# Group norm and attention over 4096 positions: the running score maxima of a chunk folded from 1024 to 256 columns before the block turn

## The reference

```python
def _L0_conv_ref(x, Wq, Wk, Wv, gamma):
    f = jnp.einsum('qc,bcn->bqn', Wq, xf)          # 64 x N
    g = jnp.einsum('qc,bcn->bqn', Wk, xf)          # 64 x N
    h = jnp.einsum('vc,bcn->bvn', Wv, xf)          # 256 x N
    scores = jnp.einsum('bqn,bqm->bnm', f, g)      # N x N
    beta = jax.nn.softmax(scores, axis=1)          # over n
    o = jnp.einsum('bvn,bnm->bvm', h, beta)
    return gamma[0] * o + xf
x = x + _L0_conv_ref(_gn(x), ...)                  # _gn: group norm, 32 groups
```

## Time and profile before

| | before |
|---|---|
| median of 3 runs | 1927.47 us (1927.34 to 1928.86) |
| the profiled execution | 1927.25 us, span of its records 1925.5 us |
| TensorE clock granted | 1.000 of full speed over the span |
| busy share of the span | PE 98%, DVE 82%, ACT 82%, POOL 68% |
| block turn, L873 | 64 instructions of 128 x 1024, 79.1 us |
| reduction, L878 | 64 instructions of 128 x 1024, 76.0 us |

### The profile page before, as it was taken

How to read it: one execution, slowest core, us unless ns; L and a number is a source line. 1 busy time by engine, 2 the same in 40 slices (tenths; PEclk the granted TensorE clock), 3 DMA queues, 4 the chain that set the end, 5 groups by cost and what they waited for, 6 DMA issues and landing times.

```text
span 1925.5 us, 44218 instructions
## 1 busy us (share of the span) xinstructions
PE 1895.5 (98%) x17497; PEld 1566.5 (81%) x17497; DVE 1587.3 (82%) x1923; ACT 1571.8 (82%) x1677; POOL 1307.2 (68%) x765
## 2 busy tenths in 40 slices
PE   6899999999999999999999999999999999999999
PEld 3678888878888888887888888888788888888888
DVE  7888998887778899987777989998777787888784
ACT  4788889977778888897877888898787788888885
POOL 4367668866656677886654766788575567766777
PEclk9999999999999999999999999999999999999999
DMA  4022112212111221211211211121130111111111
GB/s 144 4 68 77 45 33 74 56 23 64 32 41 55 74 54 28 73 53 32 60 36 40 71 52 54 53 56 45 28 72 24 23 31 32 32 25 31 32 31 37
DMA packets 200110, 91.19 MB, mean 47 GB/s; under 512 B 150240, under 2 KB 191712, under 8 KB 199904
## 3 DMA queue, kind: packets, MB, share of 16 engines
q1 hardware_dynamic: 199904, 88.36, 17.6%
HBM read 46.60 MB, written 16.78 MB: 33 GB/s over the span
## 4 chain that ended last, share of the span: by engine, by line
PE 93%; issue 0%; ACT 0%; DVE 0%; POOL 0%; DVEq 0%
PE O L515 23%; PE O L517 23%; PE O L516 23%; PE S L503 7%; PE S L500 7%; PE S L497 6%; PE O L474 1%; PE O L476 1%; PE O L475 1%; PE S L526 1%; PE O L460 1%; PE O L459 1%; PE O L464 1%; PE S L474 0%; PE S L475 0%
## 5 line engine op out<-in xcount | busy, mean ns | idle before, releaser
L400 POOL TENSOR_TENSOR PL<-SC,PH 128x1024 f16<-128x1024 f32 x511 | 1089.2, 2137 | 562.1 <-ACT SC L669 558.7
L515 PE MATMUL O<-V,PH 128*128 128x257 f16 x4096 | 1118.3, 273 | 1.2 <-POOL PL L428 1.1
L517 PE MATMUL O<-V,PL 128*128 128x257 f16 x4096 | 1118.2, 273 | 0.0
L516 PE MATMUL O<-V,PH 128*128 128x256 f16 x4096 | 1116.4, 273 | 0.0
L668 ACT ACTIVATE PH<-SC 128x1024 f16<-128x1024 f32 x511 | 539.1, 1055 | 119.0 <-PE O L517 110.8
L907 DVE TENSOR_TENSOR SC<-SC,MB 128x1024 f32<-128x1024 f32 x511 | 613.1, 1209 | 0.1
L662 ACT ACTIVATE SC<-S 128x1024 f32<-128x1024 f32 x512 | 502.8, 1013 | 117.6 <-issue 105.5
L867 DVE TENSOR_TENSOR XM<-S,XM 128x1024 f32<-128x1024 f32 x384 | 468.0, 1219 | 125.6 <-PE S L503 124.2
L669 ACT ACTIVATE SC<-SC 128x1024 f32<-128x1024 f32 x511 | 533.3, 1044 | 0.0
L515 PEld LDWEIGHTS O<-V,PH 128*128 128x128 f16 x4096 | 406.0, 99 | 49.8 <-POOL PL L428 1.3
L516 PEld LDWEIGHTS O<-V,PH 128*128 128x128 f16 x4096 | 400.8, 98 | 50.0
(11 more groups left out here) (126 smaller groups left out, 1076.1 us busy)
## 6 DMA issues: line engine op xcount, KB each, us to landing
xin<-x SPq DMA_DIRECT2D x24, 1024.0 KB, 5.6
xres<-x SPq DMA_DIRECT2D x64, 256.0 KB, 2.9
ATT<-OT SPq DMA_DIRECT2D x1008, 16.0 KB, 1.9
out<-RES SPq DMA_DIRECT2D x63, 256.0 KB, 2.2
SC<-x SPq DMA_DIRECT2D x8, 512.0 KB, 7.4
F<-GG SPq DMA_DIRECT2D x64, 64.0 KB, 2.0
GG<-GG SPq DMA_DIRECT2D x32, 128.0 KB, 2.4
SC<-wvT SPq DMA_DIRECT2D x1, 256.0 KB, 6.8
```

Source lines behind the costliest of these rows:

```text
L400: pool.tensor_tensor(PL[:, s % RING, :], sc(s), PH[:, s % RING, :], ALU.subtract).then_inc(pl_ready, 1)
L515: mm(o[:, 0:C + 1], PH[:, n % RING, cols], vh, start=t == 0, stop=False)
L516: mm(o[:, 0:C], PH[:, n % RING, cols], vl, start=False, stop=False)
L517: w = mm(o[:, 0:C + 1], PL[:, n % RING, cols], vh, start=False, stop=t == T - 1)
```

## The change

The 1024 columns of XM are folded in place by two elementwise maxima: columns 0 to 511 with 512 to 1023, then 0 to 255 with 256 to 511. Both inputs and the output of each lie in SBUF. Behind each fold DVE waits for its own result, by a new semaphore `mx_folded`. The turn then covers 256 columns instead of 1024, the tensor MT has 256 columns instead of 1024, and the reduction goes over 256 columns (32 for each of the 8 outputs) instead of 1024.

```diff
-        MT = sb("MT", [P, GW], f32)
+        MT = sb("MT", [P, M], f32)
...
+        mx_folded = sem("mx_folded")
...
             def turn_maxima(c):
                 dve.wait_ge(s_maxed, G * (c + 1))
                 if c > 0:
                     dve.wait_ge(mxq_ready, c)
-                ve.transpose(MT[:, :], XM[:, :]).then_inc(mx_turned, 1)
+                for i, w in enumerate((GW // 2, M)):
+                    ve.tensor_tensor(XM[:, 0:w], XM[:, 0:w], XM[:, w:2 * w], ALU.max).then_inc(mx_folded, 1)
+                    dve.wait_ge(mx_folded, 2 * c + i + 1)
+                ve.transpose(MT[:, :], XM[:, 0:M]).then_inc(mx_turned, 1)
 
             def quadrant_maxima(c):
 
                 dve.wait_ge(mx_turned, c + 1)
-                ve.tensor_reduce(mxq, MT[:, :].rearrange("p (i j n) -> p j i n", i=GT, j=NB), axis=AX.XY,
+                ve.tensor_reduce(mxq, MT[:, :].rearrange("p (j n) -> p j n", j=NB), axis=AX.X,
                                  op=ALU.max).then_inc(mxq_ready, 1)
```

## The result

| | before | after |
|---|---|---|
| median | 1927.47 us | 2024.92 us (2018.46 to 2028.23, 6 runs) |
| ratio, 95% interval | | 1.0501 (1.0482 to 1.0519) |
| the profiled execution | 1927.25 us, span 1925.5 | 2028.23 us, span 2026.5 |
| TensorE clock granted, mean | 1.000 | 0.988 |

The change makes the kernel 97 us slower, 5.0%; the forecast was 2014 us.

What follows compares the result with a forecast made beforehand. PE's own work was taken to bound the kernel. Boundary stalls of 37 + 31 + 20 us, less 0.9 in the opening, made 87 us on 1927.25 us: forecast 2014 us, range 1938 to 2050 us.

Steps and rivals of the forecast that it cites:

- What bounds, and where it breaks: PE's own work sets the time; a late DVE hurts first at the boundary between two chunks, at the wait for `scale_output`.
- the slack: At a chunk boundary, `scale_output`'s first half may be 1.44 us later before PE waits; 0.75 us at the six coefficient boundaries.
- The wait for POOL: On DVE, a fold waits for the rest of whatever POOL instruction is running; the bounds were nothing and that rest.
- The argument from L847: L847, with SBUF input and output, took 2.29 us instead of 0.80 behind a running POOL instruction; folds should wait likewise.
- The handover: Between the folds, POOL's waiting instruction (2.14 us at plain boundaries) gets in, and fold 2 ends about 0.22 us after it.
- plain: 44 boundaries where POOL starts L400 0.24 us after the turn began; PE stalls 0.84 us each, 37 us in all.
- 12 normalising: Boundaries where POOL runs a pair of L424, 2.12 us each, from -0.20; PE stalls 2.55 us each, 31 us in all.
- 6 coefficient: Chunks 5 and 6 of three batches, POOL's first L400 beginning 0.07 before the turn; stall 3.39 us each, 20 us.
- Fold 2 keeps its turn: Rival: DVE's next instruction precedes the waiting POOL instruction, so the folds run together; 16 us slower, 1943 us; chance 0.17.
- no wait at all: Rival: folds do not wait for POOL, PE never stalls, only the -0.9 us is left; 1926 us; chance 0.14.
- POOL's queue first: Rival: at the 12 normalising boundaries each fold lets one more POOL instruction of 2.1 us pass; 2064 us; chance 0.06.
- The gain of 0.9 us forecast for the opening: Chunks 0 and 1, where PE waits for the first weights: shorter turn and reduction save 0.45 us each.

Runs made afterwards that it cites:

- delay experiments: Kernel before, with two or four extra reductions of XM as pure delay ahead of each turn from chunk 2 on: 1989.98 us and 2235.96 us.
- the last experiment: Changed kernel with POOL held back for the turn, plus two extra reductions of MT, 0.39 us each, ahead of the real one: 1927.70 us, ratio 1.0005.
- the delay kernel: Kernel before, with two extra reductions of XM to 8 columns as pure delay ahead of each turn from chunk 2 on: 1989.98 us, ratio 1.0326.

## Why the prediction was right, point by point

**What bounds, and where it breaks.** Right. PE had 81.6 us of waits for `scale_output` at 59 boundaries, and at the other three the same wait, put down to L916 (1.9 us); none elsewhere of note. The delay experiments show that the place and the slack hold for delays of 2.4 and 4.9 us that have nothing to do with folds.

**The wait for POOL.** Right, and shown: same length and same place, 418 ns with one input in PSUM, up to 2354 with both in SBUF; holding POOL back brings both folds to 0.71 and 0.43 us. The argument from L847 led to the right end of the bounds. Its reason was looser than the fact: the runs show that one SBUF input goes free in a maximum (and in every reduction tried), and two wait. L847, which has one SBUF input and waited all the same, is another operation (a tensor_scalar), and no run here takes its case apart. The sentence of the Trainium skill, in SBUF — State Buffer, section "Who interferes with whom", that two SBUF inputs contend with a GpSimd instruction that reads SBUF, agrees with this pair of runs. The other half of what the prediction took from the Trainium skill there, that whichever starts first holds the ports for its whole length, agrees too, but for the edge: POOL got in some 0.15 us before the end of fold 1's record.

**The handover.** Right: fold 2 lost its turn to a POOL instruction at all 62 boundaries (not in the two turns of the opening), and a queued POOL instruction did not go first (the order L425, fold, L425, fold). One sign was named wrongly: L401 does not start at 0.69 but at 0.24, and the wait is inside its record. Fold 1 holds POOL up by 0.30 us, less than the 0.45 forecast, since POOL gets in some 0.15 us before fold 1's record ends.

**The sizes**, as idle time in the profile and as time lost (how much later the matmul behind the stall starts, set against the same matmul of the kernel before; at most boundaries 0.16 us more, for the matmul's modelled end):

| boundaries | forecast | idle | lost |
|---|---|---|---|
| plain | 0.84 | 0.65 | 0.82 |
| six with V work (counted as plain) | 0.84 | 1.11 | 1.27 |
| three with f and g work (counted as plain) | 0.84 | 0.64 | 0.67 |
| the first and the last (counted as plain) | 0.84 | 2.30, 2.18 | 2.33, 2.20 |
| 12 normalising | 2.55 | 2.44 | 2.60 |
| 6 coefficient | 3.39 | 3.19 to 3.33 | 3.35 to 3.49 |

Summed over all of them, 83.5 us idle and some 10 us more: 93 us lost where the forecast had 88; the first and the last boundary alone, which it counted as plain, are 2.9 us of the difference. The span grew by 101.

**Two terms were missing**, of opposite sign. The first is the clock: it was taken to stay full ("PE's busy time stays near 1895 us at full clock"), and at 11 of the 62 stalls it fell for 3.4 us (once for twice that). Each such fall made the chunk about 1.5 us longer, some 17 us in all. The spread of the runs, which the kernel before does not have, goes with it: 2018.46 us at a mean clock of 0.994, 2022.84 at 0.990, 2028.23 at 0.988.

The second is a small gap in PE's work that the forecast had at nothing. "Where it covers nothing that PE waits for" was wrong: in the kernel before, PE lost 9.6 us in all around `share_maxima`. In the changed kernel that gap is gone, 0.25 us from the matmul before to the one behind in all 61 chunks. The shorter reduction does close most of this gap where PE does not stall (the last experiment). But in the kernel with two reductions as delay, where the reduction is as long as before, the gap is gone as well, in 60 of 61 chunks:

```profile
1725.23 0.27 PE L519 MATMUL O<-V,PL 128*128 128x257 f16 x1
1725.35 0.31 PE L528 MATMUL S<-mxs,alike 128*128 128x32 f32 x2
1725.49 0.27 PE L517 MATMUL O<-V,PH 128*128 128x257 f16 x1
```

So PE's stall at the boundary is enough by itself. It puts PE's later work in the chunk back, and the maximum that frees the half of S for `share_maxima` is not as much later: in a plain chunk it ended 0.05 us behind the start of the matmul before in the kernel before, and 0.15 us ahead of it both in the delay kernel and in the changed one. Some 9 us of what the stalls cost came back in this way. No run shows that the 0.78 us saved in the reduction add anything to that in the changed kernel.

The sum is now 93 + 17 - 9 = 101 us, the growth of the span. The stalls, forecast at 88 us, were close on their own account. That the forecast as a whole lay only 11 us under the median is in part luck, since the two missing terms cancel by half.

**The rivals.** "Fold 2 keeps its turn" and "no wait at all" are excluded by fold 2's mean of 2.18 us, "POOL's queue first" by the order at the normalising boundaries. "Not slower" became true in another way, once POOL was told to wait.

**Open.** How the chip decides when the clock falls was not looked into: at normalising boundaries with the same 2.44 us of idle time it fell at some and not at others. The gain of 0.9 us forecast for the opening does not show: PE comes to the first boundary 0.40 us later than before, and the first maximum of chunk 2 starts 0.39 us later. Why was not looked into.

## What to carry to other kernels

Before putting an elementwise instruction with two SBUF inputs on VectorE, look at what GpSimd does at that moment: the instruction may cost the rest of GpSimd's instruction, and a second one right behind it a whole one more. The same work with one operand in PSUM, or as a reduction, goes free; and if GpSimd has time to spare, one wait that keeps it out of the way can turn the loss into the gain that was meant. A shorter instruction is worth what PE waits for behind it, so follow the delay and the saving separately to the next semaphore that PE, or whoever feeds it, stands at. And do not simply add small gains to large stalls: a stall can close by itself the gap that the saving was to close.

## What was not expected of the hardware

- After an idle stretch of PE of 2.4 us and more the granted clock was at its lower level for some 3.4 us in part of the cases, about 1.5 us lost each time. It fell behind single shorter stretches too: 2.30 us in the changed kernel, 2.06 with two short maxima of SBUF inputs, 1.94 with one fold and a reduction. With 62 stalls of 3.3 us and more (four reductions as delay) the mean clock was 0.953.
- A reduction of four tiles into one, reading with a stride of 256 columns (1024 to 256), took 1963 ns. One of two tiles (512 to 256, same stride) took 698, and the kernel's own, with runs of 32 columns and 8 outputs, 1188 for 1024.
- POOL's record begins before it gets at SBUF: it showed 2.44 us instead of 2.14 when fold 1 was in its way, so a wait of this kind hides in the length of an instruction, on POOL as on DVE, and not in any idle time.
